# Four attention layers on one core: denominators in one bank, Q copies first, products with V in groups of three key tiles

## The reference, cut to what matters

```python
q, k, v = x @ Wq, ctx @ Wk, ctx @ Wv              # 16 heads
logits = einsum('bhqd,bhkd->bhqk', q, k) * scale + col_bias
probs = softmax(logits, axis=-1)                  # over 1601 keys
x = einsum('bhqk,bhkd->bhqd', probs, v) @ Wo + bo + x
```

## Time and profile before

| | us |
|---|---|
| runs | 4714.9, 4718.25, 4719.78 |
| median | 4718.25 |
| profiled execution | 4720.07 |
| its span | 4718.3 |
| mean granted TensorE clock | 0.984 |
| busy: PE, PEld | 4589.1, 2838.4 |
| busy: DVE, ACT, POOL | 3178.5, 2298.2, 2652.3 |

### The profile page before, as it was taken

How to read it: one execution, slowest core, us unless ns; L and a number is a source line. 1 busy time by engine, 2 the same in 40 slices (tenths; PEclk the granted TensorE clock), 3 DMA queues, 4 the chain that set the end, 5 groups by cost and what they waited for, 6 DMA issues and landing times.

```text
span 4718.3 us, 55964 instructions
## 1 busy us (share of the span) xinstructions
PE 4589.1 (97%) x20521; PEld 2838.4 (60%) x20521; DVE 3178.5 (67%) x5069; ACT 2298.2 (49%) x4069; POOL 2652.3 (56%) x1278
## 2 busy tenths in 40 slices
PE   8999899999999989999989999999999999999999
PEld 7888765556565445555546555555556655565554
DVE  3321477777777677787846777777766777777776
ACT  3222454455455436666655544444554545454543
POOL 0000377778777601010126877787774877787775
PEclk9999999999999979999999999999999999999999
DMA  4564921222121020011124212221216212221110
GB/s 154 169 200 147 306 66 37 58 58 58 40 51 42 16 44 16 19 29 22 39 93 145 57 37 55 58 58 31 52 49 203 49 32 58 58 58 46 45 42 18
DMA packets 100242, 332.29 MB, mean 70 GB/s; under 512 B 13941, under 2 KB 32373, under 8 KB 88186
## 3 DMA queue, kind: packets, MB, share of 16 engines
q1 hardware_dynamic: 99968, 328.72, 25.6%
HBM read 191.58 MB, written 120.31 MB: 66 GB/s over the span
## 4 chain that ended last, share of the span: by engine, by line
PE 93%; DVE 5%; issue 1%; DMA 1%; ACT 1%; SPq 0%; POOL 0%; DVEq 0%; ACTq 0%
PE ST L906 14%; PE SS L887 12%; PE OA L917 12%; PE ST L907 12%; PE OB L917 11%; PE ST L1030 4%; PE OA L1038 4%; PE SS L943 4%; PE SS L1016 3%; DVE mpart L1527 2%; PE SS L929 2%; DVE R L1543 1%; PE OB L1016 1%; PE ST L962 1%; PE ST L961 1%
## 5 line engine op out<-in xcount | busy, mean ns | idle before, releaser
L790 POOL TENSOR_TENSOR acc<-acc,P 128x1024 f32<-128x1024 f32 x912 | 2184.8, 2428 | 644.1 <-DVE acc L1459 631.0
L1217 ACT ACTIVATE P<-ST 128x512 f32<-128x512 f32 (+1 forms) x2496 | 1466.8, 598 | 1297.4 <-PE ST L907 1141.7
L1432 DVE TENSOR_REDUCE mpart<-SS 128x1 f32<-128x400 f32 (+1 forms) x3072 | 1633.6, 571 | 584.4 <-PE SS L887 506.1
L887 PE MATMUL SS<-KS,QS 68*128 68x400 f32 (+1 forms) x3072 | 1036.9, 371 | 18.3 <-DMA QS<-stq 18.2
L906 PE MATMUL ST<-QX,KX 128*128 128x512 f32 (+1 forms) x2496 | 1033.0, 414 | 3.3 <-DMA QS<-mrow 1.6
L907 PE MATMUL ST<-QS,KS 69*128 69x512 f32 (+1 forms) x2496 | 989.1, 396 | 0.0
L887 PEld LDWEIGHTS SS<-KS,QS 68*128 68x128 f32 x3072 | 584.7, 190 | 223.6 <-DVE mpart L1432 22.4
L906 PEld LDWEIGHTS ST<-QX,KX 128*128 128x128 f32 (+1 forms) x2496 | 463.0, 186 | 388.7 <-issue 286.0
L917 PE MATMUL OA<-P,Vp 128*64 128x512 f32 (+1 forms) x2496 | 661.0, 606 | 0.0
L917 PE MATMUL OB<-P,Vp 128*64 128x512 f32 (+1 forms) x2496 | 644.0, 592 | 0.0
L1292 ACT ACTIVATE PG<-ST 128x512 f32<-128x512 f32 (+1 forms) x832 | 429.4, 612 | 245.6 <-PE ST L1030 245.2
(11 more groups left out here) (234 smaller groups left out, 4374.3 us busy)
## 6 DMA issues: line engine op xcount, KB each, us to landing
q_parts<-stq SPq DMA_DIRECT2D x96, 512.0 KB, 4.6
QX<-q_parts SPq DMA_DIRECT2D x96, 512.0 KB, 11.2
KX<-k_parts SPq DMA_DIRECT2D x48, 801.0 KB, 9.3
QS<-q_parts SPq DMA_DIRECT2D x45, 512.0 KB
v_tiles<-sv SPq DMA_DIRECT2D x24, 832.0 KB, 6.5
Vp<-v_tiles SPq DMA_DIRECT2D x24, 832.0 KB, 7.0
k_parts<-skh SPq DMA_DIRECT2D x48, 400.5 KB, 4.8
k_parts<-skl SPq DMA_DIRECT2D x48, 400.5 KB, 6.0
```

The source lines that it names most:

```text
L790: gp.tensor_tensor(out, out, P[0:k, slot(H, t), q, :], ALU.add).then_inc(pool_a, 1)
L887: pe.matmul(SS[at % 3][:, 0:w], QS[H % 3][0:SROWS, qt * 128:(qt + 1) * 128], KS[H % 3][0:SROWS, o:o + w], start=True, stop=True).then_inc( ...
L1217: act.activation(P[0:k, slot(H, t), j, :], ST[n % 3][0:k, :], ACT.Exp, scale=SCALE).then_inc(act_p, 1)
L1432: dve.tensor_reduce(mpart[H % 2][:, i // len(KCH), c:c + 1], SS[RING_AT["s", H, i] % 3][:, 0:w], AX.X, ALU.max).then_inc(dve_ss, 1)
```

## The change

It changes the following.

- PV has groups of three key tiles: five steps a head, of 12, 12, 12, 4 and 12 units, in all layers.
- `sums` writes four 32-row strips of one bank, for head H-1 at the end of step 0 of head H. One copy by ACT, one reciprocal by VectorE (R4, at the end of step 1), and then eight DMAs of 64 KB by SP (`spread`) that write each strip twice into R, where the divides read it. The last head of a layer keeps the old form (`last_sums`, `take_last_z`, `last_reciprocals`); its `last_sums` now stands behind the products of the last tile.
- VectorE adds tile 1 after unit 3 of step 0 and tile 2 after unit 9, instead of at the ends of steps 0 and 1.
- POOL's divides stand ahead of its adds of tiles 9 to 12 and wait for the DMAs (d_r).
- Output items stay at four a step (u < 8).
- In the Q phase SP issues the four QS copies first, as soon as ACT has written each item, and then all stores; the maxima pieces stand at items 7 to 22.

```diff
-S_FROM, S_TO = 8, 24
+S_FROM, S_TO = 7, 23
...
-PV = [range(t, min(t + 2, KT)) for t in range(0, KT, 2)]
+PV = [range(t, min(t + 3, KT)) for t in range(0, KT, 3)]
...
-    if h % 2 == 1 and h >= 3 and g < 2 and u % 2 == 0:
+    if h % 2 == 1 and h >= 3 and g < 2 and u % 2 == 0 and u < 8:
...
 def takes_sums(h, g):
-    return g == 1 and h > 0
+    return g == 0 and h > 0
...
+def z_banks(H):
+    return H + H // HEADS
...
+        def r_spread(H):
+            return 128 * (H + 1 - (H + 1) // HEADS)
...
+            def spread(H):
+                sp.wait_ge(dve_r, z_banks(H) + 1)
+                wait(sp, pool_on, 4 * H)
+                for j in range(JQ):
+                    for half in range(2):
+                        r = 64 * (j % 2) + 32 * half
+                        sp.dma_start(R[r:r + 32, j // 2, :], R4[32 * j:32 * j + 32, :]).then_inc(d_r, 16)
...
+                for q in range(JQ):
+                    sp.wait_ge(act_qh, QITEMS * l + q + 1)
+                    sp.dma_start(words(QS[H0 % 3][0:D, q * 512:q * 512 + 512]), words(stq[q][0:D, 1, :]))\
+                        .then_inc(d_s[H0 % 3], 16)
                 for q in range(QITEMS):
...
-                    if q < JQ:
-                        sp.dma_start(words(QS[H0 % 3][0:D, q * 512:q * 512 + 512]), words(stq[q][0:D, 1, :]))\
-                            .then_inc(d_s[H0 % 3], 16)
...
             def head(l, h):
                 H, end = l * HEADS + h, (BIG if l > 0 else 1) * HEADS
+                if h > 0:
+                    spread(H - 1)
                 if h + 1 < HEADS:
                     max_row(H + 1)
...
-                gp.wait_ge(dve_r, 2 * H + c + 1)
+                if H % HEADS == HEADS - 1:
+                    gp.wait_ge(dve_r, z_banks(H) + c + 1)
+                else:
+                    gp.wait_ge(d_r, r_spread(H))
...
-                    if H % HEADS > 0 and t in (7, 8, 9, 10):
+                    if H % HEADS > 0 and t >= KT - 4:
                         gp.wait_ge(pool_a, first + 2 * min(t - 3, len(pool_tiles(H % HEADS))))
-                        divide(H - 1, t - 7)
-                        gp.wait_ge(pool_on, 4 * H - 3 + t - 7)
+                        divide(H - 1, t - KT + 4)
+                        gp.wait_ge(pool_on, 4 * H + 1 + t - KT)
...
             def sums(H):
...
+                at = RING_AT["z", H, 0]
+                wait_added(pe, H, KT - 1)
+                wait_ring(pe, at)
+                for j in range(JQ):
+                    last = pe.matmul(SS[at % 3][32 * j:32 * j + 32, :], ones[:, 0:32], acc[H % 2][:, j, :],
+                                     start=True, stop=True)
+                last.then_inc(pe_z, 1)
...
-                    if h + 1 == HEADS and g + 1 == STEPS:
-                        sums(H)
                     for t in PV[g]:
                         values(H, t)
+                    if h + 1 == HEADS and g + 1 == STEPS:
+                        last_sums(H)
                     if takes_sums(h, g):
                         sums(H - 1)
...
             def take_z(H):
+                act.wait_ge(pe_z, z_banks(H) + 1)
+                wait(act, dve_r, z_banks(H))
+                copy(Zs[:, :], SS[RING_AT["z", H, 0] % 3][:, :]).then_inc(act_z, 1)
...
+            def reciprocals(H):
+                dve.wait_ge(act_z, z_banks(H) + 1)
+                wait(dve, d_r, r_spread(H - 1))
+                dve.reciprocal(R4[:, :], Zs[:, :]).then_inc(dve_r, 1)
...
                         for i in tiles:
                             s_max(H + ahead, i)
+                        if h + 1 < HEADS and g == 0 and u in (3, 9):
+                            add(H, 1 + u // 9)
...
-                    if h + 1 < HEADS:
-                        for t in dve_tiles(h)[g:g + 1]:
-                            add(H, t)
-                    else:
+                    if h + 1 == HEADS:
                         for t in PV[g]:
                             if t in dve_tiles(h):
                                 add(H, t)
-                    if h > 0 and 2 <= g < 4:
-                        reciprocals(H - 1, g - 2)
+                    if h > 0 and g == 1:
+                        reciprocals(H - 1)
```

More of the change, by code:

```diff
@@ L119, in group_o_item @@
 def group_o_item(h, g, u):
-    return 4 * g + u // 2 if h % GROUPS == 1 and h > GROUPS and g < 2 and u % 2 == 0 else None
+    return 4 * g + u // 2 if h % GROUPS == 1 and h > GROUPS and g < 2 and u in (0, 2, 4, 6) else None
 def group_q_item(h, g, u):
-    return 2 * g + u // 4 if h % GROUPS == 2 and h + GROUPS < HEADS + 2 and g < 2 and u % 4 == 1 else None
+    return 2 * g + u // 4 if h % GROUPS == 2 and h + GROUPS < HEADS + 2 and g < 2 and u in (1, 5) else None
 def ring_order():
@@ L147, in ring_order @@
                 if takes_sums(h, g):
-                    out += [("z", first + h - 1, c) for c in range(2)]
+                    out.append(("z", first + h - 1, 0))
         out += [("z", first + HEADS - 1, c) for c in range(2)]
@@ L268, in attention_layers @@
         Oraw = at("Oraw", [128, 2, 512], o)
-        Zs = at("Zs", [128, 2, 512], o + 4096)
+        Zs = at("Zs", [128, 512], o + 4096)
+        R4 = at("R4", [128, 512], o + 6144)
+        Z2 = at("Z2", [128, 2, 512], o + 4096)
         R = at("R", [128, 2, 512], o + 8192)
@@ L365, in attention_layers @@
         dve_a, pool_a = sem("dve_a"), sem("pool_a")
-        act_o, dve_r, pool_on = sem("act_o"), sem("dve_r"), sem("pool_on")
+        act_o, dve_r, d_r, pool_on = sem("act_o"), sem("dve_r"), sem("d_r"), sem("pool_on")
         pe_out, dve_out, d_out = sem("pe_out"), sem("dve_out"), sem("d_out")
@@ L410, in wait_ring @@
             if kind == "z":
-                eng.wait_ge(act_z, 2 * n + i + 1)
+                eng.wait_ge(act_z, z_banks(n) + i + 1)
             else:
@@ L606, in q_phase @@
                 if l == 2:
-                    sp.wait_ge(pe_z, 2 * H0)
+                    sp.wait_ge(pe_z, z_banks(H0))
                     load_wq(l, 1)
+                for q in range(JQ):
+                    sp.wait_ge(act_qh, QITEMS * l + q + 1)
+                    sp.dma_start(words(QS[H0 % 3][0:D, q * 512:q * 512 + 512]), words(stq[q][0:D, 1, :]))\
+                        .then_inc(d_s[H0 % 3], 16)
                 for q in range(QITEMS):
@@ L651, in head @@
                 elif H + 1 < end:
-                    sp.wait_ge(pe_z, 2 * H)
+                    sp.wait_ge(pe_z, z_banks(H))
                     load_wq(l + 1, 0)
@@ L921, in sums, with last_sums @@
             def sums(H):
-                own = range(KT - 2, KT) if H % HEADS == HEADS - 1 else []
-                wait_added(pe, H, KT - 1 - len(own))
+                at = RING_AT["z", H, 0]
[5 more added lines that the diff above has]
+                last.then_inc(pe_z, 1)
+            def last_sums(H):
+                own = range(KT - 2, KT)
+                wait_added(pe, H, own[0] - 1)
                 for c in range(2):
@@ L928, in sums @@
                         bank, j = SS[at % 3][64 * e:64 * e + 64, :], 2 * c + e
-                        last = pe.matmul(bank, ones[:, 0:64], acc[H % 2][:, j, :], start=True, stop=not own)
+                        pe.matmul(bank, ones[:, 0:64], acc[H % 2][:, j, :], start=True, stop=False)
                         for t in own:
@@ L1226, in take_z, with take_last_z @@
             def take_z(H):
+                act.wait_ge(pe_z, z_banks(H) + 1)
+                wait(act, dve_r, z_banks(H))
+                copy(Zs[:, :], SS[RING_AT["z", H, 0] % 3][:, :]).then_inc(act_z, 1)
+            def take_last_z(H):
+                act.wait_ge(dve_r, z_banks(H))
+                act.wait_ge(d_r, r_spread(H - 1))
                 for c in range(2):
-                    act.wait_ge(pe_z, 2 * H + c + 1)
-                    copy(Zs[:, c, :], SS[RING_AT["z", H, c] % 3][:, :]).then_inc(act_z, 1)
+                    act.wait_ge(pe_z, z_banks(H) + c + 1)
+                    copy(Z2[:, c, :], SS[RING_AT["z", H, c] % 3][:, :]).then_inc(act_z, 1)
             def q_phase(l):
@@ L1234, in q_phase @@
                     act.wait_ge(pe_pv, KT * H0)
-                    act.wait_ge(pe_z, 2 * H0)
+                    act.wait_ge(pe_z, z_banks(H0))
                     for j in range(JQ):
@@ L1266, in head @@
                 if h + 1 == HEADS:
-                    take_z(H)
+                    take_last_z(H)
                 take_o(H)
@@ L1278, in group_take_z @@
                 wait(act, gdve_r, h - 1)
-                copy(Zs[:, h % 2, :], GS[GRING_AT["z", h, 0] % 4][:, :]).then_inc(gact_z, 1)
+                copy(Z2[:, h % 2, :], GS[GRING_AT["z", h, 0] % 4][:, :]).then_inc(gact_z, 1)
             def group_take_o(h):
@@ L1305, in group_layer @@
                 act.wait_ge(pe_pv, KT * HEADS)
-                act.wait_ge(pe_z, 2 * HEADS)
+                act.wait_ge(pe_z, z_banks(HEADS))
                 for j in range(JQ):
@@ L1451, in add @@
                     if t == 1:
```

(14 more changed lines are left out.)

## The result

The changed kernel takes 4815.19 us (median of four runs, 4807.78 to 4835.16) against 4716.57 us for the kernel before on the same chip: a ratio of 1.0215, 95% interval 1.0183 to 1.0247. It is slower by 1.8 to 2.5%, where 4707 us, hardly a change, was forecast, and it lies outside the range (4662 to 4755).

A forecast was written before the change was run, and what follows sets the result against it. TensorE, which never waits inside a head, was taken to bound the kernel. The terms -32 - 33 + 79 + 5 - 10 - 14 - 6 = -11 gave 4709, or 4707 us for the median, range 4662 to 4755.

The forecast's parts named there:

- the term for the clock: In the big layers' heads the new wait lowers the granted clock three or four times: +5 us, ends 0 and +63.
- rival 3: The clock falls at each new wait of TensorE: +63 in place of +5, 4765 us; chance 0.10.
- One bank: Denominator sums in one bank, 32 columns wide: -0.7 us for each of 45 heads, -32 us.
- Rival 4: The narrow denominator sums don't run side by side: -32 becomes +7, 4746 us; chance 0.03.
- Groups of three: Five steps a head instead of seven, two switches between scores and products fewer in 48 heads: -33 us.
- The adds: VectorE's adds among the first step's scores make TensorE wait 1.5 us a head, about 5 in first heads: +79 us.
- Rivals 1 and 2: Adds mostly hidden, 4655 us, chance 0.22; or POOL still adding during tile 1's add, 4748 or 4783 us, chance 0.14.
- Q copies: Q copies issued ahead of the stores shorten TensorE's waits: -4.5 in two later layers, about -5 in the first, -14 us.
- POOL, divides, spread: POOL's adds and divides and SP's DMAs of the reciprocals are never late, 2 to 5 us to spare: 0.
- Grouped layer: Fewer switches -11, longer scoring phases +16, a halved wait for the reciprocal -15: -10 us, ends -25 and +15.
- First heads: In a layer's first head, 21 tiles in 12 units, both adds block: about 5 us, 3 x 5 within +79.
- Last heads: In a layer's last head the products of tile 12 go ahead of the sums: -2 in each of three layers, -6.

The follow-up runs named there:

- e1: The changed kernel with both VectorE adds behind the last unit of step 0: 4633.87 us, ratio 0.9825 to the kernel before.
- e5: e1 with the old two-bank denominators (two banks of 64 columns, two copies, two reciprocals, no small DMAs): 4664.31 us, ratio 0.9887 to the kernel before.
- e3: The kernel before with groups of three key tiles alone, both adds at the end of step 0, divides in their old place: 4794.22 us, ratio 1.0166.
- e2: e1 with three unused VectorE reciprocals (2.4 us) after unit 3 of step 0: 4811.62 us, ratio 1.0200 to the kernel before.
- e11: e2 with its three unused reciprocals after unit 3 of step 2 in place of step 0: 4871.04 us, ratio 1.0324 to the kernel before.
- e4: The kernel before with three unused VectorE reciprocals (2.4 us) after unit 3 of step 0: 4860.90 us, ratio 1.0309.

## Why the prediction was wrong

**The step that failed** is the term for the clock: "Ends: 0, and 42 x 1.5 = +63; I take +5, three or four times, as even there four in five went free." The rate was taken from the grouped layer, where three heads of fifteen fell after a wait like this one. In the big layers it was 29 of 45, and each fall lasted from 3.4 to 13.7 us, not 4. The changed kernel's span is 179 us above e1's; 45 waits of 1.7 (63.00 less 61.30) are 77 of it, a few us more in the first heads, so about 100 us went with the clock. Even the upper end of the term, +63, was too low: it let each fall cost 1.5, where 100 us in 29 heads are some 3.5 each. That was rival 3 in kind (the sign named for it, a granted clock under 1 inside the heads, is in the stretches of head 2), and its price too was low by some 40 us. The Trainium skill, page "TensorE: Matmul & The Clock Gate", section on psum-queue depth-cycling, says that frequent short idling of TensorE between groups of matmuls, while they go round PSUM banks, makes the clock swing and costs throughput. The trace agrees in kind: 235 us at half clock behind waits of 1.5 us for a bank, though here one wait in a head of 63 us was enough.

**The rest of the sum held.** Without the adds and the clock the prediction's terms give -32 - 33 - 10 - 14 - 6 = -95; e1, which has just these parts, is 87 us shorter than the kernel before (4631.5 to 4718.3). The gap is nearly the grouped layer's; what the first heads cost and the last heads gave, neither forecast at its size, about cancels, and that is luck.

- *One bank*: 0.70 a head forecast, 0.70 measured (e5 to e1). The eight narrow instructions take 1.06 us, as worked out. Rival 4 is out. The Trainium skill's page "TensorEngine Tiling (Array Packing)", Key Properties, says that a change of tiling mode drains the engine; the whole 0.34 that the prediction put on that isn't paid here, as it would have left 0.51.
- *Groups of three*: 0.68 forecast, 0.70 measured.
- *The adds*: the walk tile by tile was right (1.5 forecast, 1.46 of idle time and 1.7 longer heads; the add at 3.6 us, 2.35 long, no POOL beside it). Rivals 1 and 2 are out.
- *Q copies*: from the start of the Q phase to the first score of head 0 the changed kernel takes 5.75, 4.77 and 4.86 us less, -15.4 against -14 (e1: -13.5).
- *POOL, divides, spread* at 0: right (POOL waits for the spread in a layer's last head alone), and only because they move together, as e3 shows.
- *Grouped layer*: -1 instead of -10. An ordinary head there takes 41.7 us in both kernels: TensorE is idle for 0.8 instead of 1.5 us in it and busy for as much longer (40.9 against 40.3). That the longer scoring phases at VectorE's pace ate up the gain is likely, not tested.
- *First heads*: even with the adds out of the way they cost more than before: 71.97 against 68.17 us in the first layer, from the first score to the next head's step 0. Of these 3.8 us 2.2 come ahead of step 0, where twelve units stand instead of eight (6.22 against 3.98), units that the last head is rid of. The other 1.6 come in the steps; the likely reason, not tested, is that 21 tiles in 12 units run at VectorE's pace. With the adds and the clock a first head's steps take another 8.8 (74.5 against 65.7).
- *Last heads*: from their second group's first score to the layer's end they gain 5.9 to 7.8 us in e1, and 5.5 to 6.9 in e5, where the sums still stand ahead of the last products. About 2 us of it are the four units that went ahead of the first head, and 0.7 the two switches that another term counts; 3 to 5 are left, where 2 were forecast. As e5 gains nearly as much, the order of the sums, which the term gave as the reason, is little of it; what the rest is was not tested.

## What to carry to other kernels

Where an engine runs without a break at full clock, price a new wait at its own length plus the half-clock stretch behind it, and take the upper end: here 1.5 us of waiting brought some 2.2 us more on average. Work that must go in among short tiles belongs where few of them follow (the end of a step, beside other work), or in pieces (0.8 us at a time cost 0.7 us a head here, and no fall of the clock). When steps are made longer, move each queue's later stages (sums, reciprocals, divides) along with them before judging the step size.

## What the runs showed of the hardware

Unexpected was how steeply the granted clock answered: waits of 0.74 us on average in one place of a head left it alone in 44 of 45 heads, waits of 2.27 us brought it to half in all 45, and the same VectorE work in three pieces never did. Unexpected too was that the place matters beside the length: 26 heads in step 0 (e2), 39 in step 2 (e11), 38 in the kernel before (e4), with waits of 1.50, 1.35 and 1.49 us. These are counts of one execution each, but the mean granted clock of every run agrees: 0.964 to 0.968 in e2, 0.950 to 0.955 in e11. Which of two equal heads of one kernel falls (head 2, not head 6) stays open.
